# Four running counts of the expert routing move from VectorE to GpSimd, in seven of eight pairs

## The reference

```
logits = xf @ gate_w.T
wts, idx = jax.lax.top_k(logits, 1)          # 8 experts
wts = jax.nn.softmax(wts, axis=-1)           # one value: weight 1
comb = jnp.einsum('nke,nk->ne', jax.nn.one_hot(idx, 8), wts)
h = jax.nn.silu(einsum('nd,eid->nei', xf, w1)) * einsum('nd,eid->nei', xf, w3)
y = jnp.einsum('nei,edi->nd', h * comb[:, :, None], w2)
y = y + jax.nn.gelu(xf @ sw1.T, approximate=False) @ sw2.T
```

## Time and profile before

| | us |
|---|---|
| median of 3 runs (lowest, highest) | 672.87 (669.7, 681.77) |
| the profiled execution | 672.23 |
| its span | 670.3 |
| TensorE busy | 597.9 (89%) |
| VectorE busy | 505.3 (75%) |
| GpSimd busy | 302.3 (45%) |

### The profile page before, as it was taken

How to read it: one execution, slowest core, us unless ns; L and a number is a source line. 1 busy time by engine, 2 the same in 40 slices (tenths; PEclk the granted TensorE clock), 3 DMA queues, 4 the chain that set the end, 5 groups by cost and what they waited for, 6 DMA issues and landing times. The chain is left out here.

```text
span 670.3 us, 13330 instructions
## 1 busy us (share of the span) xinstructions
PE 597.9 (89%) x3687; PEld 480.0 (72%) x3687; DVE 505.3 (75%) x1405; ACT 282.7 (42%) x692; POOL 302.3 (45%) x304
## 2 busy tenths in 40 slices
PE   2789999999999999992699999999998449999995
PEld 1468888888888888881466777777776338888884
DVE  6979889999999888867647788778776317777773
ACT  4323333333333333312235767566767125545451
POOL 3833335555555433200224677776765602333332
PEclk9799999999999999996557998989999659999998
DMA  8303566666665444455777665645540121222210
GB/s 290 23 1 114 164 188 187 190 191 189 190 190 174 160 160 160 160 161 152 115 163 110 101 131 126 117 88 117 101 89 25 50 69 44 68 67 72 62 58 9
DMA packets 130050, 80.89 MB, mean 121 GB/s; under 512 B 69428, under 2 KB 124365, under 8 KB 130006
## 3 DMA queue, kind: packets, MB, share of 16 engines
q1 hardware_dynamic: 125432, 73.75, 42.9%
q0 software_dynamic: 3296, 6.27, 3.1%
q10 hardware_dynamic: 1278, 0.32, 0.3%
HBM read 31.53 MB, written 49.33 MB: 121 GB/s over the span
## 5 line engine op out<-in xcount | busy, mean ns | idle before, releaser
L1062 DVE SCALAR_TENSOR_TENSOR P<-PS,QN 128x512 f32<-128x512 f32 x128 | 79.4, 683 | 33.4 <-PE PS L1187 33.4
L546 DVE SCALAR_TENSOR_TENSOR Z<-PS,Vt,Z 126x128 f32<-126x128 f32 x224 | 78.6, 351 | 8.7 <-PE PS L674 0.6
L1334 POOL DMA_INDIRECT out_h<-OS,XS x39 | 38.0, 974 | 92.1 <-DVE OS L1378 91.6
L674 PE MATMUL PS<-Wh,Ah 128*126 128x512 f32 x256 | 78.7, 430 | 0.0
L332 POOL TENSOR_TENSOR INCl<-INC,INCh 126x512 fp32r<-126x512 f32 x31 | 40.1, 1293 | 74.4 <-ACT INCh L409 74.4
L674 PE MATMUL PS<-Wl,Ah 128*126 128x512 f32 x256 | 70.5, 397 | 2.2 <-DVE Wl L510 2.2
L674 PE MATMUL PS<-Wh,Al 128*126 128x512 f32 x256 | 71.1, 400 | 0.0
L674 PEld LDWEIGHTS PS<-Wl,Ah 128*126 128x126 f32 x256 | 48.0, 188 | 14.9 <-issue 2.7
L674 PEld LDWEIGHTS PS<-Wh,Al 128*126 128x126 f32 x256 | 48.3, 189 | 12.5
L449 ACT ACTIVATE XT<-PS 128x126 f32<-128x126 f32 x32 | 8.9, 277 | 108.0 <-PE PS L720 108.0
L674 PEld LDWEIGHTS PS<-Wh,Ah 128*126 128x126 f32 x256 | 44.8, 192 | 7.8 <-issue 1.5
(11 more groups left out here) (218 smaller groups left out, 1605.3 us busy)
## 6 DMA issues: line engine op xcount, KB each, us to landing
routed<-nobody SPq DMA_DIRECT2D x30, 1170.0 KB, 5.2
IM<-v_pad SPq DMA_DIRECT2D x62, 157.5 KB
XS<-routed SPq DMA_DIRECT2D x39, 130.0 KB, 2.2
WRW<-in_w SPq DMA_DIRECT2D x16, 256.0 KB, 3.1
R<-h_rows SPq DMA_DIRECT2D x16, 129.9 KB
W1l<-in_wsig SPq DMA_DIRECT2D x4, 512.0 KB, 8.6
WR<-in_w SPq DMA_DIRECT2D x8, 256.0 KB, 5.9
q_raw<-QS SPq DMA_DIRECT2D x32, 63.0 KB
```

Source lines behind the costliest of these rows:

```text
L546: ins = dve.scalar_tensor_tensor(Z[:, u], psU[h][:, d], sc, Z[:, u], ALU.mult, ALU.add)
L674: ins = pe.matmul(out, a, w, start=(n == 0), stop=(n == len(turn) - 1))
L1062: ins = dve.scalar_tensor_tensor(P[:, b, HV * h:HV * h + HV], psC[2 * pair + hb], 0.0, QN[:, g % 2, b:b + 1].broadcast_to([128, HV, SP]), ...
L1334: pool.indirect_dma_start(out_rows, bass.IndirectOffsetOnAxis(XS[:, k % XB, IDC:IDC + 1].bitcast(i32), 0), OS[:, k % 2], None, bounds_chec ...
```

## The change

The four additions to `RUN` become a function, `add_counts`. For pairs 0 to 6 GpSimd calls it in the odd step in which TensorE ranks the pair, behind `QN` and ahead of the first scatter. For pair 7 it stays on VectorE, where it was. GpSimd has no `QN` in step 15, so pair 6's counts stand there behind `LC`. The operands and their sizes stay the same.

```diff
+        def add_counts(eng, L, m):
+
+            eng.wait_ge(oh_ready, m + 1)
+            eng.wait_ge(run_ready, m + 1)
+            for t in range(4):
+                ins = eng.tensor_tensor(RUN[:, 4 * m + t + 1], RUN[:, 4 * m + t], OH[:, m % 2, t], ALU.add)
+                if t < 3:
+                    L.link(ins)
+            ins.then_inc(run_ready, 1)
...
                     pool.tensor_tensor(QN[:, w, :, 0:S], QN[:, w, :, 0:S], PQ[:, 1:2].broadcast_to([128, GB, S]), ALU.add).then_inc(qn_ready, 1)
+                if k % 2 and on((k - 3) // 2, 0, NM - 1):
+                    add_counts(pool, L, (k - 3) // 2)
                 if on(k - 4, 0, NG):
                     scatter(k - 4, 0)
...
                 dve.tensor_tensor(oh, rev, top[:].unsqueeze(2).broadcast_to([TOK, 4, E]), ALU.is_equal).then_inc(oh_ready, 1)
-                dve.wait_ge(oh_ready, m + 1)
-                dve.wait_ge(run_ready, m + 1)
-                for t in range(4):
-                    ins = dve.tensor_tensor(RUN[:, 4 * m + t + 1], RUN[:, 4 * m + t], oh[:, t], ALU.add)
-                    if t < 3:
-                        L.link(ins)
-                ins.then_inc(run_ready, 1)
+                if m == NM - 1:
+                    add_counts(dve, L, m)
```

## The result

The changed kernel takes 704.87 us (median of 5 runs, 694.83 to 719.71) against 673.1 before; the ratio is 1.0424, with a 95% interval of 1.0371 to 1.0477. Some runs of either kernel take some per cent longer at a lower granted clock, and every ratio leaves out runs over 1.5% above the fastest of their kernel, here two of the changed kernel and one of the kernel before. It is slower by 4%, where 681 us and a range of 673 to 688 were forecast. The profiled execution took 694.83 us and is the fastest of the five; its span is 693.0 us, 22.7 above the one before.

What follows compares the result with a forecast made beforehand. TensorE, busy for 89% of the span, was taken to bound the kernel. 672.2 us plus 3.7 for the wait at `rank` plus 4.8 for clock drops gave 680.7, stated as 681 us; range 673 to 688.

Steps and rivals of the forecast that it cites:

- What bounds the kernel, what is taken away: TensorE bounds; without VectorE's held additions its 1.0 us idle time ahead of `conv` shrinks to 0.25 us.
- The cost of an addition: Each eight-column addition on GpSimd takes 0.20 us; four with links make the counts ready 1.12 us behind `QN`.
- Who waits, and the first term: TensorE's `rank` waits for the counts, about 1.5 us in pairs 0 to 5; net of relief, +3.7 us.
- the list of pairs: Start of `rank` against before, pair by pair: from +1.56 in pair 4 to -0.77 in pair 2, sum +3.7 us.
- The clock term: Idle time ahead of `rank` brings four drops to 1.2 GHz of 1.2 us each: +4.8 us, between 0 and 9.6.
- dearer additions: GpSimd's additions take 0.46 us each, so the counts come 1.04 us later in all seven pairs: +7.3 us.
- The covers: GpSimd's scatters, `X2l`, SyncE's queue and VectorE's `place` come later or wait some 0.6 us, at no cost.
- Stalls without the clock: Rival: TensorE waits at `rank` with hardly a clock drop, 676 us; chance 0.25 for 674 to 678.
- Slower by over 2%: Rival: the wait at `rank` with dearer additions and more drops, 693 us at most; chance 0.15 above 686.3.
- Faster: Rival: VectorE's relief counts and `rank` does not wait, 666 us; chance 0.08 for below 674.

Runs made afterwards that it cites:

- the filled wait: The changed kernel with twelve matmuls of 256 columns on constants put ahead of `rank`'s wait in pairs 0 to 5: 675.9 us, ratio 1.0062.
- the wait alone: The kernel before, VectorE's additions kept, plus four same-size GpSimd additions behind `QN` that `rank` also waits for: 683.39 us, ratio 1.0134.
- the other two fillings: The changed kernel with six matmuls on constants ahead of the wait, 681.34 us; or with twelve behind the two ranking matmuls, 685.89 us.

## Why the prediction was wrong

**What bounds the kernel, what is taken away: right.** TensorE's idle time ahead of the convolution shrinks, VectorE's held additions are gone, and the intervals behind the rankings of pairs 0 to 2 show it once nothing else comes last (22.2 and 21.8 instead of 22.5 and 24.1 us with the counts ahead of `LC`). Only in pair 1 the idle time is 0.61 us, not the 0.25 forecast throughout.

**The cost of an addition: right.** 203 ns against the 0.20 us worked out from wider shapes; the four take 1.05 us against 1.12 with the release. The rule of the Trainium skill (GPSIMD Engine Reference, Engine selection), two times slower, does not hold for eight columns, where it would make 0.34 us: 203 against 168 ns is a factor of 1.2.

**Who waits, and the first term: right to about 1 us.** The sum of +3.7 us was for the wait at full clock, and the filled wait measures 4.2 (2.6 to 5.7). The idle times are 1.42, 1.09 and four of 1.43, none at pair 6, where 1.5 and 0.1 stood. The time from pair 0's ranking to pair 6's is the cleanest measure, since it leaves out where `middle` begins. Its rows (columns as in the earlier trace rows) are of the kernel before, the changed one in its two profiles, and the filled wait:

```profile
371.50:507.74 136.24, 130.82 (x1154) 100.05 (x1153) 107.25 (x301) 89.50 (x186) 98.63 (x100) 0.97 0.55 105
374.96:530.30 155.34, 145.52 (x1152) 108.86 (x1153) 99.32 (x274) 87.95 (x184) 102.20 (x123) 0.88 0.49 92
371.30:533.88 162.58, 153.01 (x1153) 114.44 (x1153) 99.92 (x274) 88.05 (x184) 102.12 (x123) 0.83 0.47 88
374.85:514.41 139.56, 135.85 (x1212) 104.33 (x1213) 99.13 (x274) 87.93 (x185) 102.29 (x123) 1.00 0.53 102
```

The wait without the clock is 139.56 - 136.24 = 3.3 us there, where the list of pairs has 3.7 - 1.07 = 2.6. The changed kernel's two profiles lie 15.8 and 23.0 us above the filled one.

**The clock term: wrong, and it is most of the error.** The prediction took "four drops" of 1.2 us, together 4.8, and gave 0 to 9.6 as the ends. The count was fair: three and four in the two profiles. The price was not. A drop of 1.4 us (24.91 against 23.48) came once in each profile, and the others cost 30.72 - 23.48 = 7.2 us each. In the first profile that makes 1.4 + 2 x 7.2 = 15.9 us where 4.8 stood: 11.1 of the 14.1 us by which this execution missed its 680.7. Of the rest 0.6 is the wait, and 2.4 lie ahead of pair 0's ranking, which comes 3.46 us later than before (374.96 against 371.50) where 1.07 was forecast. The second profile has the same change and ranks pair 0 at 371.30, so those 2.4 us are not the change's. The median of the five runs, 29 us above the filled wait, would be four stretches of 7.2 us, and the slowest, 44 above it, six; their profiles were not taken. The step that failed is the one that read the length of a stretch, 3.4 us, off pairs 2 and 3 and carried it to another place. In those pairs it lay on `down`, sixteen dense matmuls. Behind `rank` lie the narrow ones, and there the stretch went on through `up` and ended in the `down` of the next step.

The trace of before had a sign of this. The busy times of its start of `middle` (columns as in the earlier trace rows), which the prediction passed over:

```profile
330.00:350.00 20.00, 19.84 (x105) 12.85 (x105) 11.62 (x25) 6.28 (x14) 5.59 (x7) 0.50 0.72 164
```

TensorE is busy for 19.84 of 20 us there at 1.2 GHz, and the clock does not rise before 359.7 us, in the midst of a `down`, after an `up` at 348 to 351 had passed without effect. A stretch in this stage can last for a step or more with TensorE busy throughout; that was there to be read. With six stretches at the price measured since, the upper end is 3.7 + 6 x 7.2 = 47 us, where the prediction has 3.7 + 9.6 = 13, and 21 with dearer additions; the slowest run lies 47 us above 672.2.

**The covers: right.** `X2l`, the scatters and SyncE's queue cost nothing that the filled kernel shows. In the changed kernel VectorE waits for the ranking matmuls 3.1 us in six times, near the 0.6 each of the prediction, to no effect seen on TensorE.

**The rivals.** "Stalls without the clock", 676 us, is what the filled wait gave (675.9), as an experiment and not as the change; that it fits to the tenth is luck. "Slower by over 2%" came true with a sixth of the chance, but through the length of the stretches, not through dearer additions. "Faster" had asked for the counts to be ready at the end of `QN`; put ahead of `LC` they are, and the 666 us given there for it was measured at 666 and 667.

**What stays open.** Behind 36 waits ahead of `rank` in six profiles (0.4 to 1.5 us, pairs 0 to 5) thirteen stretches at 1.2 GHz followed, each beginning 0.7 to 3.0 us behind the ranking; behind the eighteen rankings without idle time in the three profiles of the filled wait and the counts ahead of `LC` there is none. Which of the waits it hits follows no length that I can read: three of six at 0.46 us, one of six at 0.4 to 0.8, one of six at 0.8 to 1.4, seven of twelve at 1.1 to 1.4, and one of six at that length with dense work behind it. Why one stretch lasts 3.4 and another 17 us was not tried apart either: the two of 3.4 us behind `rank` began 1.3 and 1.4 us behind it and ended ahead of `up`, the five of 17.1 began 0.7 to 0.9 us behind it.

## What to carry to other kernels

Move work off a busy engine to a place where its consumer still finds it done: the same four additions in the same step of GpSimd make the kernel about 1% faster ahead of `LC` and 4% slower behind `QN`. Where the trace shows TensorE's clock falling, price a new idle time with the longest low stretch of that stage and not with the nearest one, look at what work stands behind it, and test it by filling the wait with matmuls on constants: that told the wait from the clock here in one experiment. When an engine's small instruction shows a maximum eight times its median, moving it along the same queue can make it worse; see first what the other engine runs beside it.

## What the runs showed of the hardware

- TensorE, busy without a gap, ran at 1.2 GHz for 13.7 or 17.1 us at a time in ten places of five profiles of this stage. A wait of 0.46 us stood 2.4 to 3.0 us ahead of three of them. Those of 17.1 us cost 7.2 us (30.72 against 23.48), those of 13.7 some 5.7 (29.17 against 23.48 with the wait alone, 28.59 against 22.93 with the counts later on VectorE).
- Seventy-two matmuls without use made the changed kernel 23 us or more faster.
- VectorE's additions of two SBUF operands took 166 to 830 ns beside GpSimd's `LC` and `QN`, and up to 1377 beside `Gl`; GpSimd's own additions of that size kept to 197 to 214 ns in the changed kernel, with the filled wait and ahead of `LC`, and one of 28 took 0.3 us in each of the other two fillings.
